# A two-layer gated cross-attention block on one core: the first loads put on one queue in a new order, the first LayerNorm split in four tiles and three, and the context's rope cut in four pieces on two engines

## The reference

```
x = x + tanh(g_xattn[0]) * xattn0(layernorm(x), ctx)      # 16 heads, latent attention with rope
x = x + tanh(g_ffn[0])   * bitlinear_ffn(layernorm(x))    # ternary weights
x = x + tanh(g_xattn[1]) * xattn1(layernorm(x), ctx)
x = x + tanh(g_ffn[1])   * gelu_ffn(layernorm(x))

# xattn0, for head h of 16:
q  = rope(layernorm(x) @ Wq[h].T @ w_kc_q[h])             # 896 x 384
kv = ctx * cos + rotate_half(ctx) * sin                   # 8 x 375 x 128, shared by all heads
p  = softmax((q @ W_qr[h]) @ (kv @ W_kr[h]).T)            # 112 x 375 for each batch
x += tanh(g) * (p @ kv @ w_kc_kv[h].T) @ Wo[:, h].T
```

## Time and profile before

| | us |
|---|---|
| median of 3 runs | 1067.36 (1064.07 to 1071.56) |
| the profiled execution, its own time | 1066.92 |
| its span | 1064.8 |
| TensorE busy | 967.7 (91%) |
| VectorE, ScalarE, GpSimd busy | 660.8, 530.2, 517.6 |

### The profile page before, as it was taken

One profiled execution on the slowest core, in us unless ns is written; L12 is line 12 of the kernel. 1 busy time (PEld: TensorE's weight loads), 2 busy tenths in 40 slices (PEclk: granted clock), 3 DMA queues, 4 the chain that ended last, 5 costly groups with the idle time before them and its releaser, 6 DMA issues. The chain is left out here.

```text
span 1064.8 us, 19577 instructions
## 1 busy us (share of the span) xinstructions
PE 967.7 (91%) x6132; PEld 569.1 (53%) x6141; DVE 660.8 (62%) x1176; ACT 530.2 (50%) x1238; POOL 517.6 (49%) x651
## 2 busy tenths in 40 slices
PE   0578989999999999799998789999999979999998
PEld 0234556555565555544443557777777754444543
DVE  2669787877878787388677446666666652322012
ACT  1246656666666665400475247767777762106400
POOL 2848777776768776211334146666666651200000
PEclk9999999999999999999999689999999999998999
DMA  8113232332314111353010022221022004104001
GB/s 231 58 28 112 58 115 50 104 83 64 114 52 127 50 51 38 105 190 114 18 63 30 30 70 71 70 69 44 25 69 69 0 1 188 40 1 168 1 30 39
DMA packets 29882, 75.56 MB, mean 71 GB/s; under 512 B 4880, under 2 KB 11152, under 8 KB 27539
## 3 DMA queue, kind: packets, MB, share of 16 engines
q1 hardware_dynamic: 23488, 64.04, 18.7%
q10 hardware_dynamic: 6352, 10.97, 3.7%
HBM read 63.98 MB, written 3.68 MB: 64 GB/s over the span
## 5 line engine op out<-in xcount | busy, mean ns | idle before, releaser
L1129 POOL TENSOR_SCALAR scratch<-scratch,rinv 112x375 f32<-112x375 f32 x256 | 154.6, 617 | 146.3 <-DVE rinv L992 146.3
L866 ACT ACTIVATE scratch<-ps,mxn 112x375 f32<-112x375 f32 x256 | 144.2, 571 | 36.4 <-DVE mxn L987 35.1
L987 DVE TENSOR_REDUCE mxn<-ps 112x2 f32<-112x750 f32 x128 | 119.6, 935 | 42.0 <-PE ps L679 41.5
L730 PE MATMUL ps<-xnT,scratch 128*128 128x448 f16 x576 | 125.3, 365 | 8.0 <-DVE scratch L1064 6.0
L1110 POOL TENSOR_TENSOR scratch<-scratch 128x448 f32<-128x448 f32 x64 | 110.3, 1733 | 33.6 <-DVE scratch L1010 19.0
L717 PE MATMUL ps<-scratch,kvn_hi 125*128 125x224 f16 x768 | 119.9, 260 | 5.3 <-DVE scratch L1032 2.3
L1121 POOL TENSOR_TENSOR scratch<-scratch 128x375 f16<-128x375 f32 x128 | 115.1, 899 | 10.9
L702 PEld LDWEIGHTS ps<-ident,scratch 112*125 112x125 f32 x768 | 100.8, 188 | 35.4 <-issue 26.7
L702 PE MATMUL ps<-ident,scratch 112*125 112x112 f32 x768 | 105.3, 273 | 9.2 <-DVE scratch L1053 9.1
L1010 DVE TENSOR_TENSOR scratch<-ps,ropeq 128x448 f32<-128x448 f32 x192 | 110.0, 616 | 4.1 <-PE ps L730 2.9
L1053 DVE TENSOR_TENSOR scratch<-ps,scratch 125x672 f16<-125x672 f32 x128 | 108.7, 849 | 4.9 <-ACT scratch L876 4.9
(11 more groups left out here) (161 smaller groups left out, 1488.7 us busy)
## 6 DMA issues: line engine op xcount, KB each, us to landing
scratch<-in_wq SPq DMA_DIRECT2D x16, 512.0 KB, 4.4
scratch<-in_wo SPq DMA_DIRECT2D x16, 512.0 KB, 3.8
wabs<-in_w ACTq DMA_DIRECT2D x32, 256.0 KB, 3.0
scratch<-in_w SPq DMA_DIRECT2D x8, 1024.0 KB, 4.8
scratch<-in_W SPq DMA_DIRECT2D x8, 1024.0 KB, 6.0
scratch<-scratch SPq DMA_DIRECT2D x64, 112.0 KB, 2.2
scratch<-in_kcq SPq DMA_DIRECT2D x8, 512.0 KB, 3.5
scratch<-in_qr SPq DMA_DIRECT2D x32, 128.0 KB, 3.5
```

What stands on the lines that cost most here:

```text
L730: last = nc.tensor.matmul(out, lhs[i](c), rhs[j](c), start=(n == 0), stop=(n == 3 * chunks - 1))
L866: last = nc.scalar.activation(prob[0:S, s % 2, hh, :], scores_ps[0:S, hh, 0:L], ACT.Exp, bias=mxn[0:S, s % 2, hh:hh + 1], accum_out=rsum[0 ...
L987: nc.vector.tensor_reduce(mxn[0:S, s % 2, :], scores_ps[0:S, :, 0:L], AX_X, ALU.max, negate=True).then_inc(max_done, 1)
L1129: last = nc.gpsimd.tensor_scalar(prob[0:S, s % 2, hh, :], prob[0:S, s % 2, hh, :], rinv[0:S, s % 2, hh:hh + 1], P_SCALE, ALU.mult, ALU.mult)
```

## The change

- All first loads but the two gates go on SP's queue, one after the other: identity, tiles 0 to 3 of `x`, wq, kckv, wo, tiles 4 to 6 of `x`, the context's rope table, context of batches 0 and 1, kcq, qr, context 2 and 3, the queries' rope table, context 4 and 5, context 6 and 7, bias. Before, SP issued `x` (3 tiles), identity, `x` (4 tiles), wq, kcq, qr, kckv, wo, and ACT issued the rest at the same time.
- The first four tiles are normalised alone, with statistics, normalisation and low half of different tiles interleaved on VectorE. The other three follow inside iteration -1: their statistics after slot 2 (behind the split of wq), their normalisation after slot 3, their transposes and halves after slot 4. The normalised rows have four buffers of their own, the PSUM banks are 0 and 1 in place of 6 and 7, and A2 waits for all seven tiles.
- The rope of the context is cut in four pieces of two batches: 0 and 1, then 2 and 3, on GpSimd before iteration -1, with the last three `norm_rstd` between them; 4 and 5 on VectorE after slot 6; 6 and 7 on GpSimd after slot 6. Each piece waits for its own load and for the piece before it.
- Batches 4 to 7 of the context are transposed and split after slot 0 of iteration 0; the softmax's transposes of pair 0 wait for that. VectorE's wait for the queries' rope table moves to the first block of head 0, and the two small instructions on gates and identity to slot 6.
- Two semaphores are shared by both layers. Nothing else of layer 1 changes.

```
@@ first loads
-            sp.dma_start(x_first[:, 0:3], xt_d[:, 0:3]).then_inc(s_x[0], 16)
             sp.dma_start(ident[:, :], tab["ident"]).then_inc(s_ident, 16)
-            sp.dma_start(x_first[:, 3:NT], xt_d[:, 3:NT]).then_inc(s_x[1], 16)
-            load_pair(sp, 0, 0)
+            sp.dma_start(x_first[:, 0:N_FIRST], xt_d[:, 0:N_FIRST]).then_inc(s_x[0], 16)
+            load_pair(sp, 0, 0, names=("wq", "kckv", "wo"))
+            sp.dma_start(x_first[:, N_FIRST:NT], xt_d[:, N_FIRST:NT]).then_inc(s_x[1], 16)
+            for lo, hi in KV_ROWS:
+                sp.dma_start(ropek[lo:hi], tab["ropek"][lo:hi]).then_inc(s_ropek, 16)
+            load_ctx(sp, 0)
+            load_pair(sp, 0, 0, names=("kcq", "qr"))
+            load_ctx(sp, 2)
+            sp.dma_start(ropeq[:, 0:5, :], tab["ropeq"][:, 0:5, :]).then_inc(s_ropeq, 16)
...
+            load_ctx(sp, 4)
+            load_ctx(sp, 6)
+            sp.dma_start(bias0[:, :], w["bias0"]).then_inc(s_bias0, 16)
@@ start_scalar
-            for lo, hi in KV_ROWS:
-                act.dma_start(ropek[lo:hi], tab["ropek"][lo:hi]).then_inc(s_kv, 16)
-                act.dma_start(kvraw[lo:hi], w["ctx"][lo:hi]).then_inc(s_kv, 16)
-            act.dma_start(ropeq[:, 0:5, :], tab["ropeq"][:, 0:5, :]).then_inc(s_ropeq, 16)
...
-            for t in range(NT):
-                norm_high(act, n0, t, 6 + t % 2)
+            for t in range(N_FIRST):
+                norm_high(act, n0, t, t % 2)
@@ the context's rope
-            pool.wait_ge(s_kv, 64)
-            for c in range(LC):
-                nc.gpsimd.tensor_tensor(kvn[0:LP, :, c, :], kvraw[0:LP, :, c, :], ...)
-                for lo, hi in ((0, DC // 2), (DC // 2, 0)):
-                    last = nc.gpsimd.tensor_tensor(kvt[0:LP, :, c, lo:lo + DC // 2], ...)
+        def kv_rope(eng, op, b):
+            if b == 0:
+                eng.wait_ge(s_ropek, 32)
+            eng.wait_ge(s_kv[b // 2], 32)
+            if b > 0:
+                eng.wait_ge(kv_roped, b // 2)
+            op.tensor_tensor(kvn[0:LP, b:b + 2], kvraw[0:LP, b:b + 2], ..., ALU.mult)
+            for lo, hi in ((0, DC // 2), (DC // 2, 0)):
+                last = op.tensor_tensor(kvt[0:LP, b:b + 2, :, lo:lo + DC // 2], ..., ALU.mult)
             last.then_inc(kv_chain, 1)
-            pool.wait_ge(kv_chain, 1)
-            for b in range(0, B, 2):
-                nc.gpsimd.tensor_tensor(kvn[0:LP, b:b + 2], kvn[0:LP, b:b + 2], ...)
+            eng.wait_ge(kv_chain, b // 2 + 1)
+            op.tensor_tensor(kvn[0:LP, b:b + 2], kvn[0:LP, b:b + 2],
+                             kvt[0:LP, b:b + 2], ALU.add).then_inc(kv_roped, 1)
@@ VectorE's start
-            for t in range(NT):
-                if t == 3:
-                    dve.wait_ge(s_x[1], 16)
-                norm_stats(dve, n0, t, x_first)
-            for t in range(NT + 2):
-                if t < NT:
-                    norm_apply(dve, n0, t, x_first)
-                if t >= 2:
-                    norm_low(dve, n0, t - 2, 6 + t % 2)
+            for t in range(N_FIRST + 2):
+                if t < N_FIRST:
+                    norm_stats(dve, n0, t, x_first)
+                if 0 <= t - 1 < N_FIRST:
+                    norm_apply(dve, n0, t - 1, x_first)
+                if t >= 2:
+                    norm_low(dve, n0, t - 2, t % 2)
@@ where the context's batches go
-            kv_behind = {5: (0, 1), 6: (2, 3, 4), 7: (5, 6, 7)}
+            kv_behind = {(-1, 5): (0, 1), (-1, 6): (2, 3), (0, 0): (4, 5, 6, 7)}
+            rope_behind = {(-1, 6): 6}
+            LATE = (2, 3, 4)
@@ TensorE: group(), iteration(), turn()
-                        if layer == 0 and first(p) and g == ("A", 0):
-                            pe.wait_ge(n0.low, (HALF + P - 1) // P)
+                        if layer == 0 and first(p) and g in (("A", 0), ("A", 2)):
+                            pe.wait_ge(n0.low, N_FIRST if n == 0 else NT)
...
+                            if layer == 0 and first(p) and s == LATE[2]:
+                                for t in range(N_FIRST, NT):
+                                    norm_turn(pe, n0, t, t % 2, n0.low, banks=2)
...
+                        if layer == 0 and isinstance(p, int) and p == 0 and s == 0:
+                            pe.wait_ge(kv_low, B)
@@ VectorE: iteration()
+                            if layer == 0 and first(p) and s == LATE[0]:
+                                start_vector_late(dve)
+                            if layer == 0 and first(p) and s == LATE[1]:
+                                for t in range(N_FIRST, NT):
+                                    norm_apply(dve, n0, t, x_first)
+                            if layer == 0 and first(p) and s == LATE[2]:
+                                for t in range(N_FIRST, NT):
+                                    norm_low(dve, n0, t, t % 2)
+                            if layer == 0 and first(p) and s == 6:
+                                kv_rope(dve, nc.vector, 4)
+                                start_vector_small(dve)
@@ GpSimd
+                            if layer == 0 and isinstance(p, int) and (p, s) in rope_behind:
+                                kv_rope(pool, nc.gpsimd, rope_behind[p, s])
...
                         start_gpsimd(pool)
-                        pool.wait_ge(n0.turned, NT)
+                        kv_rope(pool, nc.gpsimd, 0)
+                        for t in range(N_FIRST, NT):
+                            norm_rstd(pool, n0, t)
+                        kv_rope(pool, nc.gpsimd, 2)
```

More of the change, by code:

```diff
@@ L261, in flamingo, with load_pair @@
         s_gate = sem("gates_done")
[L263 to L266 removed]
+        def load_pair(sp, layer, q, free=None, names=("qr", "kcq", "wq", "kckv", "wo")):
+            for n in names:
                 src = w[f"{n}{layer}"][ds(q, 1)]
@@ L434, in kv_turn @@
         def kv_turn(pe, b):
-            pe.wait_ge(n0.low, NT)
             pe.wait_ge(kv_roped, b // 2 + 1)
```

93 lines of the change are left out of this document (51 added, 42 removed).

## The result

| | median us (range, runs) | ratio to before [95%] |
|---|---|---|
| before | 1067.83 (1064.07 to 1071.56, 4) | |
| after | 1051.57 (1049.37 to 1053.76, 4) | 0.9863 [0.9833, 0.9893] |

The change makes the kernel 1.4% faster. The profiled execution took 1053.55 us, with a span of 1051.8; the forecast against the same kind of number was 1053.1.

What follows compares the result with a forecast made beforehand. TensorE is 90% busy or more nearly everywhere, so time could be won only in its idle start. The terms sum to -13.85 us at the second scores; against the profiled 1066.92 this gives 1053.1 us, range 1046 to 1061.

Steps and rivals of the forecast that it cites:

- Up to A0: Start of the kernel: loads, four tiles' normalisation and wq's split let A0 start at 19.8 us, 21.15 us earlier.
- A0 to first B: TensorE from A0 to the first B: same 7.33 us as before, A0 keeping 4.64; change 0.
- late normalisations: VectorE ahead of B's rope: three normalisations delay that rope, for which A1 waits; +2.3 us, bounds 1.6 and 5.8.
- late transposes and halves: Behind A1, ahead of head 0's block 1: three tiles' transposes and halves, +3.8 us; 2.6 at full clock.
- slots 5 to 7: Rope behind A1 to C0: one context batch less, but VectorE's rope piece 3 delays GpSimd's sums 2.8 us; +0.4 us.
- C0 to first scores: Batches 5, 6 and 7 no longer stand between C0 and first scores: 3.9 us in place of 6.39, -2.5.
- iteration 0: First to second scores: context batches 4 to 7 now stand behind A3 on TensorE, +3.3 us.
- Rival 2: At the start, loads land later than the curve or lose their order: 1057 to 1058, or 1060 us; chance 0.22.
- rival 3: At the start, one queue carries only part of two queues' rate: 1063, or a loss at 1072 us; chance 0.07.
- the other rule: VectorE's rope piece 3 beside GpSimd's sums: exclusive port lock makes them add to 6.1 us, about 1 us worse.
- Rival 1: A0, A1 and late transposes run at 2.4 GHz, plus catching up: 1047 to 1049 us; chance 0.21.
- Nothing moves behind iteration 0: After the second scores the shift carries to the end; possible catching up of 0 to 2 us taken as nothing.

Runs made afterwards that it cites:

- run 2: Kernel after with the loads in the order and on the two queues of the kernel before: 1052.84 us, 0.9872 of before.
- run 3: Kernel after, same load order, but tables, context and bias on ACT's queue: 1050.84 us, 0.9857 of before.
- run 8: Kernel after with tiles 2 and 3 of x issued on ACT's queue ahead of the gates: 1051.85 us, 0.9858 of before.
- run 9: Kernel after with the gates' two loads issued only once the first tiles of x have landed: 1057.33 us, one run.
- run 1: Kernel before with all first loads but the gates on SP's queue in order of need: 1056.73 us, 0.9912 of before.
- run 6: Kernel after with the three late normalisations on VectorE moved behind the rope that frees A1's bank: 1046.43 us, 0.9809 of before.
- run 5: Kernel after with the context's rope piece 3 on GpSimd in place of VectorE: 1051.68 us, 0.9862 of before.
- run 7: Kernel after with unread dummy transposes of the identity where TensorE would wait: 1045.63 us, 0.9827 of before.

## Why the prediction was right, and where two errors met

Each term against the marks of the two profiled executions:

| term | predicted | measured |
|---|---|---|
| A0 | -21.15 | -18.90 |
| A0 to first B | 0 | +0.49 |
| late normalisations (B to A1) | +2.3 | +3.20 |
| late transposes and halves (A1 to the rope behind it) | +3.8 | +3.45 |
| slots 5 to 7 (that rope to C0) | +0.4 | -0.33 |
| C0 to first scores | -2.5 | -1.46 |
| iteration 0 (first to second scores) | +3.3 | +3.21 |
| sum at the second scores | -13.85 | -10.34 |
| behind them | 0 | -2.1 up to the 57th scores (1.7 of it in iteration 1), -0.9 behind these |

The last column ends at -13.4, from 1066.92 to 1053.55. The prediction had the direction, the size and the mechanism; its sum was 3.5 us too good at the second scores and lacked the 3.0 us behind them, 1.7 of which an alignment gave in iteration 1. The agreement of the totals to 0.5 us is luck to that extent. Two of the terms that look right are so by luck as well: A0 to first B, and the late transposes.

**Up to A0: mis-sized by 2.25.** Of this 1.46 is the landing of the first four tiles, predicted 7.8 and measured 9.26 (9.10 again). The step was to read each landing off before's curve, as if only the order of the bytes changed. But before, 2 to 6 us moved 62 and then 304 GB/s, after 94 and 120. The windows of the kernel before:

```profile
2.00:4.00 2.00, 0.00 (x0) 0.00 (x0) 0.00 (x0) 0.00 (x0) 0.00 (x0) 1.00 0.34 62
4.00:6.00 2.00, 0.00 (x0) 0.00 (x0) 0.00 (x0) 0.00 (x0) 0.00 (x0) 1.00 0.81 304
```

Runs 2, 3, 8 and 9 locate it: two queues for the later pieces change nothing (9.34), the four tiles ahead of the identity land at 7.90, `x` on ACT's queue ahead of the gates lands at 7.25, gates issued only behind `x` let it land at 6.69. As far as these runs go, it takes both, the identity ahead and the gates beside. The other 0.8 is in the walk from there to A0, 12.8 us in place of 12.0 (11.3 as walked and 0.7 added), and it is one instruction: the low half of wq was taken at 1.2 us and took 2.15, beside GpSimd's first rope piece. In the second trace of after it meets the same piece and takes 1.23, and A0 comes at 20.97, which is its landing of 9.10 and a walk of 11.9. From VectorE's timeline of that trace:

```profile
19.60 1.23 DVE L1100 SCALAR_TENSOR_TENSOR scratch<-scratch 128x1024 f16<-128x1024 f32 x1 [0.30 <-ACT scratch L955]
```
The later landings held: the first context piece was predicted for 18.9 and GpSimd's first multiplication starts at 19.02 (17.89 in the second trace), from its timeline:

```profile
19.02 1.81 POOL L416 TENSOR_TENSOR arena<-arena 125x768 f32<-125x768 f32 x1 [2.74 <-DMA arena<-in_ctx]
```

**What brings A0 forward was credited too much to the order of the loads.** The text has one walk with both; runs 1 and 2 part them: order alone gives A0 at 30.81, placement alone at 23.07, both at 22.05. The placement alone carries it; the queue and the order add 0.2 us at the 57th scores over run 2 (1.3 by the second trace of after), the queue alone 1 to 2 over run 3. Rival 2 and rival 3, later loads and one slow queue, are ruled out: kcq is there at 21.13 (20.5 predicted), where ScalarE waits 1.4 us for it but would have stood until A0's end anyway, no later context piece is waited for, and the windows show 244 GB/s at the least from 8 to 26 us.

**A0 to first B: right in sum, by cancelling.** A0 took 4.07 in place of 4.64, but the low half of kcq took 2.32 beside GpSimd's rope where I had kept 1.25. The B behind it took 2.40 in place of 1.34, which cost nothing here, as its rope came only at 33.86 behind the late normalisations. I had looked at how before's B ran (full pace) and not at the gap ahead of it: before 2.69 us, now 3.76. In the second trace of before the same B took 2.40 behind a gap of 3.17, so its full pace was itself one execution's.

**Late normalisations: the mechanism right, the size off by 0.9.** They took 4.29 us, 1.21, 1.21 and 2.02, where I had 0.9 to 1.1 each; the bounds of 1.6 to 5.8 hold it. Run 6 shows that the place costs 3.2 us at A1, and 2.1 more up to the second scores through TensorE's pace, which the prediction did not connect with it. The powers came as walked (25.55 to 27.14, predicted 24.9 to 26.5) and were no wait.

**Late transposes: right in sum, by cancelling.** I had taken them at half pace. They ran at full pace: eight in 1.04 us (the row at 39.29), where before's took 1.09 for four. The prediction's own figure for that is 2.6. The rest is A1 itself, 4.40 us in place of 3.69, which I had taken as unchanged; 2.6 and 0.7 are 3.3 of the 3.45.

**Iteration 0: right** within 0.1 us.

**Slots 5 to 7: 0.7 better, by a cost put on the wrong engine.** I had GpSimd's two sums end 2.8 us later than alone. They took 3.88 in place of 3.18, 0.7 more, and C0 stands right behind them (54.13 after 54.03); before it came 1.8 us behind them, in TensorE's own queue. The 2.8 us fell on VectorE, in the next stretch.

**C0 to first scores: mis-sized by 1.0, and here the other rule won.** I took 2.9 us for VectorE's piece 3; it took 5.73 (51.06 to 56.79), and the low halves behind it are what the scores wait for. GpSimd's two sums lie beside it:

```profile
50.15 3.88 POOL L1157 TENSOR_TENSOR scratch<-scratch 128x448 f32<-128x448 f32 x2 [3.49 <-DMA scratch<-scratch]
```

Alone they take 3.18. The two pieces of work took 6.6 us from 50.15 to 56.79, where 2.9 and 3.2 one after the other are 6.1; GpSimd's split of K0 lies in these 6.6 us as well. The single instructions show it better. GpSimd's second sum ends at 54.03, and VectorE's multiplication, begun in the middle of it, ends 0.4 us behind that, having taken 2.43 us where I had 0.5:

```profile
51.24 2.79 POOL L1157 TENSOR_TENSOR scratch<-scratch 128x896 f32<-128x896 f32 x1
52.02 2.43 DVE L420 TENSOR_TENSOR arena<-arena 125x384 f32<-125x384 f32 x1
```

The Trainium skill (SBUF — State Buffer, section on the two separate sides) has it so: VectorE's instructions with two inputs in SBUF and GpSimd's that read SBUF exclude each other, and the sum by its rule was 6.1. The trace agrees: the one that came second ends only behind the other. The row of L458, by which I chose, shows four instructions that met GpSimd only in part; it doesn't price a full meeting. Where it costs is at the first scores; run 5 shows that three batches later it is neutral.

**Rival 1 was real, and won in part.** Of its clock terms, 2.2 for A0, 1.2 for A1 and 1.5 for the late transposes, the last came true without any help. The other two, 3.4 together, are what run 7 finds when TensorE is kept busy: 1.64 and 1.96. My argument against it, that the gaps ahead of A0 remain, was what the trace showed (3.95 us); the one ahead of A1 even grew, from 0.64 to 2.79.

**Nothing moves behind iteration 0** failed in the small. I took nothing for catching up between 80 and 92 us, and nothing was gained there; the 2.1 us from there to the 57th scores were not in view at all.

Left open: whether the 0.9 us behind the 57th scores (0.4 of them outside the span), and the 3 us by which the medians differ more than the profiled executions (16.3 against 13.4), are more than the scatter of the half-clock passages in the middle. The traces of after have 222.09 and 218.55 there, those of before 220.68 and 216.09, so nothing in them points to the change. The interval of the ratio, 0.9833 to 0.9893, is 11 to 18 us and holds the 12.45 and the 13.4.

## What to carry to other kernels

When a start is shortened, ask separately what must be loaded and what must be computed before the first dependent work: here the new placement, with four tiles in place of seven ahead of A0, did nearly all, and ordering the loads, good for 8 us alone, added 0.2 to 1.3 us to it. Work put in an empty place on VectorE is only as cheap as GpSimd's instructions beside it allow: behind the rope the same three normalisations cost 1.45 us, ahead of it 4.29. And after a gain at the start, look at whether TensorE's remaining gaps now leave it at half rate; here filling them with work that nothing reads won 6.3 us, 3.6 of them in the matmuls themselves, as much as the best edit of the order. And when a term of a forecast comes out right, look at its parts before believing it: the late transposes, forecast as 3.8 and measured as 3.45, were made of other things than forecast.

## What the runs showed of the hardware

**Half rate under a full granted clock.** A0's window after reads 1.00 granted, and yet its 12 matmuls took 4.07 us, 0.34 each, where the same 12 take 2.43 behind idle turns. Only a later window, 28.5 to 38.7, reads 0.52. Both of the kernel after:

```profile
22.00:26.20 4.20, 4.07 (x12) 1.57 (x12) 2.71 (x9) 0.00 (x0) 4.12 (x5) 1.00 1.08 262
28.50:38.70 10.20, 6.04 (x16) 2.21 (x17) 7.56 (x8) 0.00 (x0) 6.45 (x7) 0.52 0.28 79
```

With idle turns the window over A1 reads 1.00 and A1 takes 2.44 us. At this start the duration of a matmul tells the rate, the granted clock doesn't.

**Who comes first pays least, when VectorE and GpSimd meet.** In the kernel before VectorE's low half of wq starts 0.1 us behind GpSimd's second sum and takes 3.05 us, where the same instruction takes 1.24 to 1.26 in the five pairs behind. In the kernel after it starts 0.3 us ahead of that sum and takes 1.37, and the sum takes 3.06 in place of 2.08. Two executions of the kernel after show the same with nothing changed. In one GpSimd's first piece starts at 19.02, VectorE's low half of wq at 19.76, in the middle of the first multiplication, and takes 2.15 us. In the other the piece starts at 17.89; the low half comes at 19.60, just ahead of GpSimd's second multiplication (19.65), and takes 1.23. GpSimd's second and third multiplications are stretched in both, to 2.94 and 2.98 us from the 1.95 that they take in the last piece, at 58.69. A0 stands 1.08 us apart in the two. From GpSimd's timelines, the first line of the first trace, the others of the second:

```profile
20.78 2.94 POOL L420 TENSOR_TENSOR arena<-arena 125x384 f32<-125x384 f32 x2
...
17.89 1.81 POOL L416 TENSOR_TENSOR arena<-arena 125x768 f32<-125x768 f32 x1 [1.78 <-DMA arena<-in_ctx]
19.65 2.98 POOL L420 TENSOR_TENSOR arena<-arena 125x384 f32<-125x384 f32 x2
```

So a microsecond of jitter in a landing decides whether VectorE, for which A0 waits, is held as well.

**Two 1 KB loads slow a 1 MB one.** With the gates' loads spread over 128 partitions beside it and the identity ahead of it, the first load moved 94 and 120 GB/s from 2 to 6 us; with these issued behind it, 182 and 349 (one execution). With the gates beside it but the 1 MB load first on its queue (run 2) it was there at 7.90 in place of 9.34 (run 3).
